# Four GNN layers in one kernel: where the row copies run, and work moved beside two loops

## What is computed

```python
h = maximum(layernorm(x), 0)                      # layer 0: attention with 4 heads
ht = (h @ Wm).reshape(n, 4, 64)
scores = leaky_relu(el[:, :, None] + er.T[None], 0.2), masked by adj
x = x + softmax(scores) @ ht
h = maximum(layernorm(x), 0)                      # layer 1, adj without its diagonal
node_support = adj0 @ h
edge_output = gru_cell(node_support, h, ...)      # "edge stage"
for i in range(3):                                # three attention heads
    hW = h @ W[i];  e = leaky_relu((adj0 @ hW) @ a_i)
    edge_support += softmax(where(adj0 > 0, e, -inf)) @ hW
node_output = gru_cell(edge_support / 3, h, ...)
x = x + d * edge_output + d * node_output         # d: the diagonal
```

## Time and profile before

| what | us |
|---|---|
| median of 3 runs (1324.97 to 1328.03) | 1327.91 |
| the profiled execution | 1326.06 |
| its span, first to last instruction | 1324.0 |
| TensorE matmuls busy in it | 1139.3 |
| VectorE busy | 937.4 |
| ScalarE busy | 784.3 |
| aggregation of layer 0, first to last matmul | 92.95 to 387.25 |
| turning loop of layer 1 | 399.88 to 420.7 |
| edge stage | 464 to 690 |

### The profile page before, as it was taken

One profiled execution on the slowest core, in us unless ns is written; L12 is line 12 of the kernel. 1 busy time (PEld: TensorE's weight loads), 2 busy tenths in 40 slices (PEclk: granted clock), 3 DMA queues, 4 the chain that ended last, 5 costly groups with the idle time before them and its releaser, 6 DMA issues.

```text
span 1324.0 us, 35106 instructions
## 1 busy us (share of the span) xinstructions
PE 1139.3 (86%) x15054; PEld 937.7 (71%) x15054; DVE 937.4 (71%) x2037; ACT 784.3 (59%) x1001; POOL 228.1 (17%) x296
## 2 busy tenths in 40 slices
PE   4519898888866989999978999999999997778997
PEld 3418898888865766666656888888888654446886
DVE  5786677767995299999986998769995365553541
ACT  3479988778825123333327999989989365653000
POOL 5631011111103012222222000001220141220000
PEclk9759899999995889999989999999999998999999
DMA  9936567879518334433337345318852000020532
GB/s 217 179 52 68 63 73 115 117 108 133 71 3 293 101 100 124 116 114 111 106 111 223 106 143 197 114 59 294 286 186 104 5 29 17 16 96 1 189 118 87
DMA packets 128083, 153.77 MB, mean 116 GB/s; under 512 B 32065, under 2 KB 105393, under 8 KB 127665
## 3 DMA queue, kind: packets, MB, share of 16 engines
q1 hardware_dynamic: 74993, 127.05, 30.4%
q0 software_dynamic: 51744, 23.88, 15.8%
q10 hardware_dynamic: 1184, 0.53, 0.1%
HBM read 171.26 MB, written 35.60 MB: 156 GB/s over the span
## 4 chain that ended last, share of the span: by engine, by line
PE 54%; DVE 23%; issue 8%; ACT 6%; POOL 4%; DMA 3%; SPq 0%; DVEq 0%; POOLq 0%; ACTq 0%
PE PS L1620 18%; PE PS L1761 10%; PE PS L1762 9%; DVE scratch L1317 9%; PE PS L1815 8%; PE PS L1711 3%; POOL arena L704 2%; PE PS L1802 2%; DVE arena L1299 2%; DVE arena L1091 2%; PE PS L1718 1%; DVE arena L1343 1%; PE PS L1655 1%; DMA arena<-e_rows 1%; DMA arena<-in_edge_WhhT 1%
## 5 line engine op out<-in xcount | busy, mean ns | idle before, releaser
L1761 PE MATMUL PS<-arena 128*128 128x257 f16 x1452 | 325.3, 272 | 7.0 <-ACT arena L898 4.1
L1762 PE MATMUL PS<-arena 128*128 128x257 f16 x1452 | 325.3, 274 | 0.0
L1620 PE MATMUL PS<-arena 128*128 128x65 f16 x7744 | 260.1, 196 | 74.7 <-DVE arena L1137 40.4
L1620 PEld LDWEIGHTS PS<-arena 128*128 128x128 fp8e4 x7744 | 256.7, 99 | 78.0 <-issue 77.4
L812 ACT ACTIVATE arena<-arena 128x1408 fp8e4<-128x1408 f32 x176 | 241.9, 1456 | 45.9 <-DVE arena L1131 45.7
L1317 DVE CUSTOM_DVE_ANT_0 scratch<-arena 128x1408 bf16<-128x1408 bf16 x132 | 223.1, 1690 | 23.2 <-DMA arena<-e_rows 10.8
L898 ACT ACTIVATE arena<-arena 128x896 int16<-128x896 uint8 (+1 forms) x198 | 187.0, 971 | 22.1 <-DVE arena L1372 14.2
L1761 PEld LDWEIGHTS PS<-arena 128*128 128x128 bf16 x1452 | 142.7, 98 | 31.0 <-issue 8.2
L1762 PEld LDWEIGHTS PS<-arena 128*128 128x128 bf16 x1452 | 139.9, 96 | 21.5
L1131 DVE TENSOR_TENSOR arena<-arena,AT 128x352 int32<-128x352 int32 x176 | 91.2, 518 | 78.0 <-PE PS L1620 59.7
L889 ACT ACTIVATE arena<-arena,E1B 128x896 uint8<-128x896 f32 (+1 forms) x131 | 139.1, 1063 | 1.7 <-DMA arena<-m_rows 1.7
(11 more groups left out here) (189 smaller groups left out, 1338.3 us busy)
## 6 DMA issues: line engine op xcount, KB each, us to landing
arena<-adj_rows_half SPq DMA_DIRECT2D x88, 352.0 KB, 3.0
arena<-in_adj SPq DMA_DIRECT2D x44, 704.0 KB, 4.4
adj_rows_half<-in_adj POOLq DMA_DIRECT2D x22, 704.0 KB, 11.9
hw_saved<-arena SPq DMA_DIRECT2D x22, 387.0 KB, 4.2
AT<-in_adjT POOLq DMA_DIRECT2D x44, 176.0 KB, 8.3
arena<-hw_saved SPq DMA_DIRECT2D x9, 774.0 KB, 6.6
arena<-el_rows SPq DMA_DIRECT2D x8, 704.0 KB, 10.3
arena<-h_saved SPq DMA_DIRECT2D x44, 128.0 KB, 2.1
```

The source lines that it names most:

```text
L1620: ins = pe.matmul(PS[:, first_bank(n) + i, (2 * r + q) * C0:(2 * r + q + 1) * C0], MASK[:, (m + j) % NMASK, q, k * P:(k + 1) * P], MOV[:, ...
L1761: pe.matmul(PS[:, k, 0:D + 1], weights, w[:, 0:D + 1], start=(j == 0), stop=False)
L1762: ins = pe.matmul(PS[:, k, 0:D + 1], weights, w[:, D + 2:2 * D + 3], start=False, stop=(j == NT - 1))
```

## The change

**Row copies.** The 22 copies leave layer 0. Copies 0 to 3 are issued by POOL within its cast loop (at blocks 12, 15, 18, 21), copy 4 behind it, and copy t + 5 at the head of step t of the edge stage. Each waits until the copy three before it has landed; a copy is cut into pieces of a quarter row, not an eighth. SP zeroes the diagonal per block (`clear_diagonal`): blocks 0 to 3 before the first row loads, block t + 4 in step t behind the row loads; ahead of the row loads of a step it waits for the clears so far.

**Thresholds.** The first six thresholds of layer 0 are made in ScalarE's loop of operand halves, one behind each of blocks 14 to 19.

**First support product.** `support(0, 0)` and `support(0, 1)` are made in the turning loop of layer 1, block by block (four matmuls each), and their halves are taken right behind it. The fillers are now `support(1, c)`, and the first two steps of the edge stage have no support product.

The changed lines (context left out):

```diff
+    THR_AT = 14
...
+    ROWS_LEAD = 5
...
-        ZB = a0.take(NT, dt=BF16, size=2)
...
-        assert NREAL <= (P - 1) * NT
...
-        NOTI = sb("NOTI", [P, P])
+        NOTI = sb("NOTI", [P, P], BF16)
+        ZB = sb("ZB", [P, 2], BF16)
...
+        copy_sems = [("adj_a", NT), ("adj_b", NT), ("rows_h", 0)]
+        def row_copied(t):
+            name, before = copy_sems[t % 3]
+            return sem(name), 16 * (before + t // 3 + 1)
...
-            sp.wait_ge(sem("rows_h"), 16 * NT)
-            sp.dma_start(AH_D.rearrange("t p n -> (t p n)")[0:(P - 1) * NT * (N + 1)]
-                         .rearrange("(a b c) -> a b c", b=NT, c=N + 1)[:, :, 0:1],
-                         ZB[0:P - 1, :].unsqueeze(2), allow_slow_non_contiguous=True).then_inc(sem("rows_z"), 16)
-            sp.wait_ge(sem("rows_z"), 16)
...
+            def clear_diagonal(t):
+                n = P if t < NT - 1 else P - 1
+                sp.wait_ge(*row_copied(t))
+                sp.dma_start(AH_D.rearrange("t p n -> (t p n)")[t * P * (N + 1):(t * P + n) * (N + 1)]
+                             .rearrange("(a c) -> a c", c=N + 1)[:, 0:1],
+                             ZB[0:n, 0:1], allow_slow_non_contiguous=True).then_inc(sem("rows_z"), 16)
...
+            for t in range(ROWS_LEAD - 1):
+                clear_diagonal(t)
+            sp.wait_ge(sem("rows_z"), 16 * (ROWS_LEAD - 1))
...
+                if 1 <= t and t + ROWS_LEAD - 2 < NT:
+                    sp.wait_ge(sem("rows_z"), 16 * (t + ROWS_LEAD - 1))
+                    assert half_of(L)[0] <= t + ROWS_LEAD - 2 or t + ROWS_LEAD - 2 >= NT - 1
+                if t + ROWS_LEAD - 1 < NT:
+                    clear_diagonal(t + ROWS_LEAD - 1)
...
-            link(pool.memset(ZB, 0.0))
+            link(pool.memset(ZB[:], 0.0))
...
-            for t in range(NT):
-                pool.wait_ge(sem("masks_built"), 68 + 4 * t)
-                pool.dma_start(AH_D[t].rearrange("p (c n) -> c p n", c=8),
-                               t_in["adj"][t * P:(t + 1) * P, :].rearrange("p (c n) -> c p n", c=8)).then_inc(sem("rows_h"), 16)
+            def copy_row(t):
+                if t >= 3:
+                    pool.wait_ge(*row_copied(t - 3))
+                pool.dma_start(AH_D[t].rearrange("p (c n) -> c p n", c=4),
+                               t_in["adj"][t * P:(t + 1) * P, :].rearrange("p (c n) -> c p n", c=4)
+                               ).then_inc(row_copied(t)[0], 16)
+                if t >= 12 and t % 3 == 0:
+                    copy_row(t // 3 - 4)
+            copy_row(ROWS_LEAD - 1)
...
+                if t + ROWS_LEAD < NT:
+                    copy_row(t + ROWS_LEAD)
...
-            for t in range(NT):
-                act.wait_ge(sem("t_b"), t + 1)
-                act.wait_ge(sem("t_d"), t + 1)
-                act.activation(MOV[:, t, :, 0, :], TS[:, t % 3, :].rearrange("p (h c) -> p h c", c=C0), ACT.Copy
-                               ).then_inc(sem("mov_hi"), 1)
...
-            act.wait_ge(sem("mov"), NT)
-            act.wait_ge(sem("u_mm"), 1)
+            for t in range(NT):
+                act.wait_ge(sem("t_b"), t + 1)
+                act.wait_ge(sem("t_d"), t + 1)
+                act.activation(MOV[:, t, :, 0, :], TS[:, t % 3, :].rearrange("p (h c) -> p h c", c=C0), ACT.Copy
+                               ).then_inc(sem("mov_hi"), 1)
+                if t == THR_AT:
+                    act.wait_ge(sem("u_mm"), 1)
+                    act.wait_ge(sem("elb0"), 16)
+                if THR_AT <= t < THR_AT + NTHR:
+                    threshold(0, t - THR_AT)
-                    threshold(n, j)
+                    if n > 0 or j >= NTHR:
+                        threshold(n, j)
...
-            act.wait_ge(sem("fr_arg"), 1)
-            act.activation(FR, FR, ACT.Exp).then_inc(sem("fr"), 1)
+            for c in range(DC):
+                support_high(0, c)
+            act.wait_ge(sem("fr_arg"), 1)
+            act.activation(FR, FR, ACT.Exp).then_inc(sem("fr"), 1)
...
-            for c in range(DC):
-                support_high(0, c)
...
+            def support_low(s, c):
+                dve.wait_ge(sem("ns_hi"), DC * s + c + 1)
+                dve.tensor_tensor(NSH[:, s % 2, c, 1, :], PS[:, c, 0:D], NSH[:, s % 2, c, 0, :],
+                                  ALU.subtract).then_inc(sem("ns_lo"), 1)
+            for c in range(DC):
+                support_low(0, c)
...
-            def support_low(s, c):
-                dve.wait_ge(sem("ns_hi"), DC * s + c + 1)
-                dve.tensor_tensor(NSH[:, s % 2, c, 1, :], PS[:, c, 0:D], NSH[:, s % 2, c, 0, :],
-                                  ALU.subtract).then_inc(sem("ns_lo"), 1)
...
-            for c in range(DC):
-                support_low(0, c)
...
+            def support(s, c, j0=0, j1=NT):
+                i0, i1 = SUP[s]
+                if s >= 1 and j0 == 0:
+                    pe.wait_ge(sem("ns_lo"), DC * (s - 1) + c + 1)
+                for j in range(j0, j1):
+                    for a in range(2):
+                        ins = pe.matmul(PS[:, c, 0:D], HHL[:, j, a, c * P:(c + 1) * P],
+                                        AT[:, j, i0 * P:i1 * P], start=(j == 0 and a == 0), stop=(j == NT - 1 and a == 1))
+                if j1 == NT:
+                    ins.then_inc(sem("ns"), 1)
+            pe.wait_ge(sem("diag0"), DIAG0)
...
+                support(0, 0, t, t + 1)
+                support(0, 1, t, t + 1)
-            pe.wait_ge(sem("diag0"), DIAG0)
-            def support(s, c, j0=0, j1=NT):
-                i0, i1 = SUP[s]
-                if s >= 1 and j0 == 0:
-                    pe.wait_ge(sem("ns_lo"), DC * (s - 1) + c + 1)
-                for j in range(j0, j1):
-                    for a in range(2):
-                        ins = pe.matmul(PS[:, c, 0:D], HHL[:, j, a, c * P:(c + 1) * P],
-                                        AT[:, j, i0 * P:i1 * P], start=(j == 0 and a == 0), stop=(j == NT - 1 and a == 1))
-                if j1 == NT:
-                    ins.then_inc(sem("ns"), 1)
...
-            support(0, 0, 0, 11)
+            support(1, 0, 0, 11)
-            support(0, 0, 11, NT)
+            support(1, 0, 11, NT)
-            support(0, 1, 0, 14)
+            support(1, 1, 0, 14)
-            support(0, 1, 14, NT)
+            support(1, 1, 14, NT)
...
-                if s + 1 < len(SUP):
+                if 2 <= s + 1 < len(SUP):
```

More of the change, by code:

```diff
@@ L1669, in support @@
                     ins.then_inc(sem("ns"), 1)
+            l1_transposes(0)
+            pe.wait_ge(sem("diag0"), DIAG0)
+            for t in range(NT):
+                if t + 1 < NT:
+                    l1_transposes(t + 1)
+                pe.wait_ge(sem("hts_dve" if t % 2 == 0 else "hts_act"), t // 2 + 1)
+                for c in range(DC):
+                    for a, b in TERMS:
+                        ins = pe.matmul(PS[:, 5, t * H1:(t + 1) * H1], HTS[:, t, (DC * a + c) * P:(DC * a + c + 1) * P],
+                                        U1S[:, c, b, 0:H1], start=(c == 0 and a + b == 0), stop=(c == DC - 1 and a == 1))
+                ins.then_inc(sem("hu_mm"), 1)
+                support(0, 0, t, t + 1)
+                support(0, 1, t, t + 1)
+            pe.wait_ge(sem("up"), 1)
+            for t in range(NT):
+                for j in range(NT):
+                    ins = pe.matmul(PS[:, 4, t * 10:(t + 1) * 10], AT[:, j, t * P:(t + 1) * P], UP[:, j, :],
+                                    start=(j == 0), stop=(j == NT - 1))
+            ins.then_inc(sem("e_mm"), 1)
             def products(t):
```

16 lines of the change are left out of this document (removed).

## The result

The changed kernel took **1339.54 us** (median of 4 runs, 1335.32 to 1343.39) against 1326.44 us (4 runs, 1320.50 to 1328.03) for the kernel before: a ratio of 1.0106, 95% interval 1.006 to 1.0152. The forecast was 1311 us, with a range from 1299 to 1328. The time moved the other way.

A forecast was written before the change was run, and what follows sets the result against it. Layer 0's aggregation was bound by TensorE, losing 32.8 us mostly to code waits behind row copies; the edge stage by VectorE. Terms -25 - 0.7 + 4 + 1.5 + 2.5 + 1 = -16.7 us gave 1311 us, range 1299 to 1328.

The forecast's parts named there:

- Part 1: Row copies out of layer 0: TensorE's gaps in the aggregation mostly go, -25 us, between 13 and 31 gained.
- The open term: Layer 0: four gaps beside score loads (13.4 us) and the half clock after gaps (6.2 us); 7.6 us taken to stay.
- The end moves with TensorE: End of layer 0: VectorE, with 12 masks of room (17 us), stays ahead, so TensorE sets the end.
- Part 2: Six thresholds beside the operand halves on ScalarE: layer 0's aggregation starts near 92.2 us, -0.7 us (-2 to +1).
- The feared table loads in turn: ScalarE alternating Copy and Sigmoid: a load at each change would cost 10 x 1.28 = 13 us; not counted.
- Part 3: First support product in layer 1's turning loop: +4 us at full clock, +14 at half clock.
- Part 4: Copies and clears in layer 1's front and edge stage: +1.5 us score loads, +2.5 ten-column products, +1 edge stage.
- (d): Edge stage: row loads come late for VectorE's maxima, from a landing of about 5 us on; 1361 us, chance 0.11.
- (e): Front of layer 1: SP or POOL, in order, hold each other; front ends 15 us later, 1324 us, chance 0.07.
- (b): Layer 0: score loads cause the gaps, copies are bystanders; Part 1 gives 13 us, 1323 us, chance 0.10.
- (a): Layer 0: score loads alone make no gap; residual 1.6 instead of 7.6 us, 1305 us, chance 0.13.
- (c): Layer 1's turning loop stays at half clock: +14 instead of +4 us, 1321 us, chance 0.12.

The follow-up runs named there:

- before_rows: Kernel before, its copies still in layer 0 but as whole rows, row index outermost, instead of eighths: 1334.58 us, ratio 1.0032.
- before_16: Kernel before, its copies still in layer 0 but cut into sixteenths instead of eighths: 1327.61 us, ratio 0.9959.
- copies_16: Kernel before with only the row copies moved as in the change, cut into sixteenths; no early thresholds, no moved support product: 1308.15 us, ratio 0.9823.
- cut8: Changed kernel with its row copies cut into eighths of a row instead of quarters: 1317.80 us, ratio 0.9913.
- cut16: Changed kernel with its row copies cut into sixteenths of a row instead of quarters: 1307.30 us, ratio 0.9842.
- parts_2_3: Kernel before plus the six early thresholds and the first support product in the turning loop; copies and clear stay in layer 0: 1326.79 us, ratio 0.9959.
- one_copy: Changed kernel with one row copy and one clear (block 0) instead of 22, all row loads reading block 0: 1302.34 us, ratio 0.9805.
- cut32: Changed kernel with its row copies cut into thirty-seconds of a row instead of quarters: 1368.22 us, ratio 1.0279.

## Why the prediction was wrong, step by step

**Part 1, right.** Forecast -25 us, measured -27.7 at the last aggregation matmul (387.25 to 359.57), of it 1.2 before the first one. From first to last matmul that is 294.3 to 267.8 us; the ten versions without these copies in layer 0 took 262.5 to 271.0, 266.1 on average, a gain of 28; one execution tells it to some 4 us. The open term, what a score load does alone, was taken at 6 + 1.6 = 7.6 us of gaps left; 5.1 us are left. The half clock after gaps went almost wholly (0.99 granted). That the copies make the gaps is shown: they leave, and the gaps with them; before_rows makes them longer. That the gaps are waits for code fits their place between groups of 128 matmuls, but no run tests it apart. "The end moves with TensorE" was not quite so: TensorE has caught up with VectorE, and waits once for a mask in the last 6 us (0.26 us, the last row under layer 0 above) in every version with the copies moved.

**Part 2, right.** Forecast -0.7, measured -1.15 (92.95 to 91.80), of which 0.3 is chance: where the loop of operand halves stands varies by several us between executions. From ScalarE's copy of block 14 to the first matmul it is 19.7 us in before, before_16 and copies_16, and 18.9 in the changed kernel, cut8, cut16 and parts_2_3: Part 2 gives 0.8 us. The feared table loads in turn didn't come; one stands before the first Sigmoid, none between the pairs (ScalarE's timeline, against the earlier trace rows):

```profile
73.55 1.28 ACT L833 ACT_TABLE_LOAD   x1
74.85 1.47 ACT L833 ACTIVATE arena<-arena 128x1408 fp8e4<-128x1408 f32 x1
76.22 0.63 ACT L839 ACTIVATE arena<-arena 128x520 f16<-128x520 f32 x1
```

**Part 3, +4 forecast, about 0 measured.** The choice of the row with full clock was right: the clock is 0.50 in the first 6 us of the loop and 1.00 after.

```profile
373.00:379.00 6.00, 5.56 (x57) 4.58 (x58) 2.73 (x9) 3.03 (x6) 1.11 (x3) 0.50 0.88 284
379.00:396.00 17.00, 15.27 (x248) 12.77 (x245) 10.40 (x25) 12.37 (x24) 9.99 (x19) 1.00 0.96 234
```

The rest was too much: at full clock a block is 0.86 us of TensorE (14 matmuls; 248 in 15.27 us), forecast 0.94, and the loop went at 0.95 us a block before, so the added matmuls fit into time in which TensorE had waited for ScalarE, POOL and VectorE (parts_2_3: 0.1 us). The 2.1 us by which the loop grew belong to Part 4, most likely to POOL issuing copies between its casts, and in my working those three issues cost nothing. The pause of 13.77 us ahead of the loop, for 12.63, is in every version that has the copies moved and in none that hasn't. It is VectorE's: with the gaps gone it ends its mask work closer to TensorE's end (L1240 starts 3.8 us before that end; before, as L1209, 5.0 us), and all that follows on it is as long as it was.

**Part 4, the step that failed.** The pass L1700: +2.5 forecast, +2.3 measured, which is luck in part, since the other cuts make it +4.1 (cut8) and +5.3 (cut16). The rest of it was costed with "a copy took 5.6 us of all 16 engines" and with its landing of 11.9 us, both of the earlier trace rows, for a copy cut in eighths. The diff cuts it in quarters, and that edit, plain in its lines, was costed at nothing. The 5.6 us of engine time held (5.0 measured), but by the rule above it lies on four engines now, and the landing became 20.8 us. Three numbers of Part 4 fell with it:
- "SP goes on near 438 us, and `et` is due near 450 plus the delays above, so SP's wait itself is hidden". Layer 0 ended some 26 us sooner, so these are 412 and 424 us of the changed kernel. `et` was ready near 427, but SP went on at 430.5, after copy 0, copy 3 behind it and a clear. The cover that I named was gone. For that case I had priced SP's wait at what it exceeds (here 4.4 us), and not the store of the turned h that it pushes right ahead of the e_rows store (1.44 to 10.40 us). Together +12.0 for +1.5.
- "A copy is over two steps old when SP's clear waits for it": at 21.3 us, with steps of some 12 us, it is not always. In the edge stage SP stood 8.6 us ahead of clears waiting for copies, and 21.9 us ahead of row loads waiting for clears to land, a wait that had no price at all; in cut16 the two are 0 and 8.8 us.
- The landing of a row load, "3.0 x 1.6 = 4.8 still fits": it was 6.2, past the 5 us from which rival (d) decides.

SP's two waits in the second point, from 455 to 710 us of the changed kernel:

```profile
SPq L498 <- DMA adj_rows_half<-ZB: 21.9, 11, 4.4
...
SPq L490 <- DMA adj_rows_half<-in_adj: 8.6, 3, 4.3
```

The cut is not all of it. cut8 is the kernel whose copies are cut as the rows' were. It took 0.87% less than before, where 1.3% was forecast, and the range holds it; but its edge stage still grew by 9.7 us for the +1 (0 to 9) of Part 4, with row loads landing in 5.7 us. So of the 26.6 us, 17 come from the quarters and 9 to 10 from a term that was too small even for eighths.

**The rivals.** (d), slower through late row loads, is what happened, at 26.6 us where I gave it 50: the landing was 6.2 and not 7.4 us, and 18 of 42 loads were waited for. (e) happened too, 12 us where I gave it 15. I gave each a chance by itself (0.11 and 0.07) and never both, though they have one cause, the time that a copy takes. With all else as forecast, (e) alone would have stayed in the range (1311 + 10.5) and (d) alone would have left it (1311 + 25.6, past 1328). (b), score loads as the cause, is false: without copies beside them the long gaps shrink to 1.21 and 2.27 us. (a), no gap from score loads alone, would have left 1.6 us, the forecast 7.6; 5.1 are left, between the two. (c), half clock in the loop, is false.

**What held with the cut mended.** cut16 took 1307.3 us, which is 17.8 less than before in the profiled executions, for a forecast sum of -16.7. By stretches it isn't as good as that: -27.7, +5.3, -2.1, +4.7 and +2.1 for -21.7, +2.5, +1.5, +1 and 0. Beside copies that run at full rate the pass L1700 has three issue gaps, 7.5 us in all (20.7 us, one_copy 12.7).

**Open.** Whether a row load is late because it shares just the four engines of a copy with it is argued, not shown; no view here gives the load of a single DMA engine. The end of layer 0 scatters by some 9 us between profiled executions with the same code there (356.55 us in cut16, 365.77 in one_copy): its first matmul starts between 91.8 and 96.3 us, and the issue gaps beside the adjacency loads before 190 us are 5.5 to 11.7 us. So differences of a few us between versions are told from their stretches above, not from totals.

## What to carry to other kernels

Before taking over a transfer's duration from a row, compare its access pattern in the diff with the one behind the row, the outermost dimension above all: the same bytes in equally many packets took 20.8, 13.4 or 9.8 us. Moving work off a place where nobody waits for it makes its latency count, so re-price the latency, not only the throughput, and re-tune the cut for the new place. And where two rivals have the same cause, give them a joint case.

## What the runs showed of the hardware

- A software DMA of 704 KB from DRAM to DRAM with 4, 8 or 16 pieces outermost (51744 packets in each kernel) lands in 20.8, 13.4 and 9.8 us; with 32 pieces, 96800 packets, in 14.8; by whole rows, 7392 packets, in 7.8.
- A store of 33 KB takes 1.4 to 1.5 us to land by itself, and 10.40 or 11.19 us when it is issued 0.4 to 0.6 us behind one of 2816 KB (10.6 to 12 us) on the same queue; 9.4 us behind it (cut32) it took 2.92 us, 10.5 us behind (cut8) 1.52.
- Issuing one such copy holds POOL for 1.0 to 1.2 us with 2064 packets, for 1.6 with the 4112 of thirty-two pieces and for about 0.5 by whole rows (48 packets).
- TensorE's issue gaps, read as waits for code, grow with the length of the packets beside them: 32.8 us with sixteenths, 43.4 with whole rows, of the same bytes.
- Six Sigmoids among Copies on ScalarE have one table load, 1.28 us ahead of the first, and none between.
